# Writing out the engine loops of a graph network's three edge layers with constant addresses and waits

## The chip, the cores and the metric

The kernel runs on one core of one Trainium2 chip. The metric is the device time of one launch, in microseconds (us): lower is better. Three runs of the kernel before gave 8099.27, 8096.51 and 8084.9 us, median 8096.51 us. The profile below is of a further execution, which took 8076.82 us.

## The reference

`x` is 3125 nodes by 128 features. There are 100000 edges `src -> dst`, sorted by `dst`, with 16 attributes and one weight each. Four graph networks run one after the other, each followed by a residual addition and a layer normalization: two attention convolutions, a mean aggregation, three edge layers, and a last attention layer. The change touches the third network alone:

```python
h = x @ W_enc + b_enc
ea = edge_attr @ W_ee + b_ee
for i in range(3):
    m = relu(h[src] + ea) * edge_atten
    aggr = segment_sum(m, dst, num_segments=n)
    z = (1.0 + eps[i]) * h + aggr
    z = z @ W1[i] + b1[i]
    z = (z - bn_mean[i]) * rsqrt(bn_var[i] + 1e-5) * bn_gamma[i] + bn_beta[i]
    h = relu(relu(z) @ W2[i] + b2[i])
```

## The kernel before, in words

The launch is a row of blocks. Up to about 3868 us come the index work, the two attention convolutions, the mean aggregation and the preparation of the edge layers. Then `gine_edges()` (line 1181) and `gine_nodes(layer)` (line 1282) alternate three times (lines 1523 and 1524), and the last network and the output follow. `gine_edges()` is the same code in all three layers.

One edge layer lays the 100000 edges on 128 partitions by J = 784 columns, so that a column is 128 edges and each partition holds edges that follow each other in `dst` order. Four columns are a quad (196 of them, `QUADS`), sixteen are a turn of the loops (`RUN` = 16, 49 turns). Five instruction streams work side by side:

- POOL (`@block.gpsimd`, line 1199) gathers, one column per indirect DMA, the rows `h[src]` from the DRAM table `h_tab` into a ring of 16 columns, that is 4 quads. Before quad q it waits until DVE has used quad q - 4 (`z_done`, q - 3). This stream is written out in full already, 784 gathers per layer.
- ACT copies a 128 by 128 block of edge attributes (line 1217) and, after PE has transposed it (line 1231), copies it back from PSUM (line 1220). PE multiplies the block with `W_ee` laid out for 8 columns (line 1235), two matrix products for two quads. The quad's bank is free again when DVE has used it.
- DVE, line 1263: waits for the quad's gather and its product and adds them into `z`, 128 by 512.
- DVE, line 1268, one per column: `m = max(z, 0) * weight`.
- DVE, line 1256, one per column: a running sum along the partition, `run = run_before * same + m`, where `same` is 0 at the first edge of a node. Each waits for the one before it (`run_done`) and for its `m` (`m_done`). The running sums of a quad are issued between the `m` operations of the quad after it.
- SP (line 1208) writes each 8 finished columns, 512 KB, to `run_tab` in DRAM. DVE waits for that before it uses the 8 places again (`run_out`).

The order on DVE is written by hand: `step(i, u, behind)` is one quad, `runs(i, u, k)` one running sum. DVE writes out the first four quads (the call `step(0, u, u > 0)`) and then runs a loop (`Fori`, line 1272) of 48 turns of four quads. SP loops over all 49 turns (line 1205), ACT and PE over turns 1 to 48 (lines 1222 and 1237). Inside a loop the turn's number is a register: addresses (`bass.ds(...)`) and the values that waits compare with are worked out by register instructions of the engine's own queue. `later()` (its wait is at line 77) is a wait that is left out where its constant is 0 or less.

The node stage that follows reads the running sum of each node's last edge from `run_tab` and applies the two products of the layer.

Of the kernel before, what the change touches and what calls it, by code (L numbers as in the profile page):

```python
# [17 lines left out]
ALU = mybir.AluOpType  # L18
# [3 lines left out]
P = 128  # L22
N = 3125
E = 100000
D = 128
# [6 lines left out]
J = -(-E // (P * 16)) * 16  # L32
# [47 lines left out]
def build(nc, a, out):  # L80
    ctx = ExitStack()
    with ctx:
# [1098 lines left out]
        def gine_edges():  # L1181

            with ExitStack() as ph:
# [7 lines left out]
                with nc.Block() as block:  # L1191
# [10 lines left out]

                    @block.sync
                    def _(sp):
                        with nc.sync.Fori(0, J // RUN) as i:
                            for h in range(2):
                                sp.wait_ge(run_done, RUN * i + 8 * h + 8)
                                sp.dma_start(run_rows[:, bass.ds((RUN * i + 8 * h) * D, 8 * D)], run[:, 8 * h * D:8 * (h + 1) * D]).then_inc(run_out[h], 16)
                        for h in range(2):
                            sp.wait_ge(run_out[h], 16 * J // RUN)  # L1210

                    @block.scalar
                    def _(act):
                        def sixteen(i):
                            for u in range(2):
                                later(act, tr_done, 2 * i + u - 1)
                                nc.scalar.copy(stage[u], ea_nat[:, bass.ds((2 * i + u) * P, P)]).then_inc(staged, 1)
                                act.wait_ge(tr_done, 2 * i + u + 1)
                                later(act, mm_done, 4 * i + 2 * u - 2)
                                nc.scalar.copy(ea_T[u], bank[6 + u][:, 0:P]).then_inc(copied, 1)  # L1220
                        sixteen(0)
                        with nc.scalar.Fori(1, J // RUN) as i:
                            sixteen(i)

                    @block.tensor
                    def _(pe):
                        def sixteen(i):
                            for u in range(2):
                                pe.wait_ge(staged, 2 * i + u + 1)
                                later(pe, copied, 2 * i + u - 1)  # L1230
                                nc.tensor.transpose(bank[6 + u][:, 0:P], stage[u], ident[:, :]).then_inc(tr_done, 1)
                                pe.wait_ge(copied, 2 * i + u + 1)
                                later(pe, z_done, 4 * i + 2 * u - 2)
                                for k in range(2):
                                    nc.tensor.matmul(bank[2 * u + k][:, :], ea_T[u], w_blocks[:, k * 512:(k + 1) * 512], start=True, stop=True).then_inc(mm_done, 1)  # L1235
                        sixteen(0)
                        with nc.tensor.Fori(1, J // RUN) as i:
                            sixteen(i)

                    @block.vector  # L1240
                    def _(dve):
# [6 lines left out]
                        def runs(i, u, k):  # L1248

                            t = 16 * i + 4 * u + k  # L1250
                            slot = 4 * u + k
                            dve.wait_ge(m_done, t + 1)
                            later(dve, run_done, t)
                            if k == 0 and u % 2 == 0:
                                later(dve, run_out[u // 2], 16 * i)
                            nc.vector.scalar_tensor_tensor(run[:, slot * D:(slot + 1) * D], run[:, (slot - 1) % RUN * D:((slot - 1) % RUN + 1) * D],  # L1256
                                                           same_nat[:, bass.ds(t, 1)], m_of(u)[:, k * D:(k + 1) * D], ALU.mult, ALU.add).then_inc(run_done, 1)

                        def step(i, u, behind):
                            q = 4 * i + u  # L1260
                            dve.wait_ge(slot_in[u], 64 * (i + 1))
                            dve.wait_ge(mm_done, q + 1)
                            nc.vector.tensor_tensor(z_of(u), bank[u][:, :], ring[:, u * 512:(u + 1) * 512], ALU.add).then_inc(z_done, 1)  # L1263
                            for k in range(4):
                                if behind:
                                    runs(i if u > 0 else i - 1, (u - 1) % 4, k)
                                dve.wait_ge(z_done, q + 1)
                                nc.vector.tensor_scalar(m_of(u)[:, k * D:(k + 1) * D], z_of(u)[:, k * D:(k + 1) * D], 0.0,  # L1268
                                                        weight_nat[:, bass.ds(16 * i + 4 * u + k, 1)], ALU.max, ALU.mult).then_inc(m_done, 1)
                        for u in range(4):  # L1270
                            step(0, u, u > 0)
                        with nc.vector.Fori(1, J // RUN) as i:
                            for u in range(4):
                                step(i, u, True)
                        for k in range(4):
                            runs(J // RUN - 1, 3, k)

# [361 lines left out]
```

## Time and profile before

| what | us |
|---|---|
| median of three runs | 8096.51 |
| the profiled execution | 8076.82 |
| its span in the trace | 8075.1 |
| edge layer 1, first gather to last running sum | 3869.5 to 5059.6 |
| edge layer 2 | 5138.5 to 6328.5 |
| edge layer 3 | 6404.3 to 7587.3 |
| busy in the span: DVE / POOL / PE / ACT | 4330.2 / 4213.9 / 3659.2 / 866.8 |

Busy time counts the work on an engine's datapath. Register, branch and wait instructions are not busy: they stand in the trace under the engine's queue, with a q behind its name (DVEq, SPq). Idle time ahead of an instruction is put down to whoever ended it. "issue" means that the profile shows nobody: the instruction was not there yet.

### The profile page before, as it was taken

Reading aid. Unit: us, or ns where it says so; the run is one execution under the profiler, and the core shown is the slowest. Engines: PE = TensorE matmul, PEld = TensorE weight load, DVE = VectorE, ACT = ScalarE, POOL = GpSimd, SP = SyncE. Lnnn points to the kernel's source line nnn. Section 1 sums busy time; section 2 is a strip of 40 time slices with the busy share of each in tenths; the row PEclk is TensorE's granted clock in tenths of the full one; section 3 lists DMA queues with packets and bytes.
Section 4 is the critical chain, followed back from the end, with each engine's and each line's share of the span. In section 5 each row is a group of like instructions: output and inputs, shape, how many; then the busy total and the mean of one; then the engine's idle time right before and its main releaser. Section 6 shows DMA issues by size and latency. Waiting matters only on the chain. (4 is left out here: it accounts for less than half of the span.)

```text
span 8075.1 us, 75499 instructions
## 1 busy us (share of the span) xinstructions
PE 3659.2 (45%) x15737; PEld 2363.8 (29%) x15739; DVE 4330.2 (54%) x9443; ACT 866.8 (11%) x2809; POOL 4213.9 (52%) x4279
## 2 busy tenths in 40 slices
PE   4366666663666666655222322332322323322244
PEld 2254444442444444455110101111110101100144
DVE  5455555554555555576444444344444344544478
ACT  0011111110111111101000000000000000000043
POOL 0455555533555555410566666466666466666443
PEclk7555555565555555577556555565566665566677
DMA  1454555524555454364322222222222222222264
GB/s 30 138 147 141 145 149 145 146 79 122 149 145 145 142 148 140 109 258 168 100 85 87 88 85 87 69 89 85 87 87 85 70 87 85 90 86 87 65 238 187
DMA packets 571997, 943.76 MB, mean 117 GB/s; under 512 B 90581, under 2 KB 413611, under 8 KB 558680
## 3 DMA queue, kind: packets, MB, share of 16 engines
q0 software_dynamic: 173728, 545.15, 22.4%
q1 hardware_dynamic: 398008, 395.34, 15.7%
q8 instruction: 139, 2.28, 0.1%
q14 instruction: 122, 1.00, 0.0%
HBM read 619.47 MB, written 320.66 MB: 116 GB/s over the span
## 5 line engine op out<-in xcount | busy, mean ns | idle before, releaser
L1199 POOL DMA_INDIRECT big<-h_tab,big x2352 | 2237.8, 951 | 1420.0 <-issue 799.3
L622 POOL DMA_INDIRECT big<-kv_tab,big x1664 | 1617.4, 972 | 1330.7 <-DVE big L788 867.6
L1235 PE MATMUL psum<-big 128*128 128x512 f32 x1176 | 969.8, 973 | 2505.4 <-DVE big L1263 2062.1
L1256 DVE SCALAR_TENSOR_TENSOR big<-big 128x128 f32<-128x128 f32 x2352 | 827.2, 352 | 1274.0 <-issue 1233.8
L1235 PEld LDWEIGHTS psum<-big 128*128 128x128 f32 x1176 | 308.5, 290 | 3013.9 <-issue 2253.8
L740 PE MATMUL psum<-big 128*128 128x136 f32 x3328 | 931.4, 433 | 488.8 <-issue 417.1
L740 PEld LDWEIGHTS psum<-big 128*128 128x128 f32 x3328 | 781.9, 315 | 642.2 <-issue 605.1
L696 PE MATMUL psum<-big 128*128 x4992 | 713.3, 296 | 408.9 <-issue 408.7
L1268 DVE TENSOR_SCALAR big<-big 128x128 f32<-128x128 f32 x2352 | 718.0, 306 | 311.3 <-issue 261.8
L783 DVE TENSOR_TENSOR big<-psum,big 128x512 f32<-128x512 f32 x416 | 287.5, 691 | 851.9 <-PE psum L696 554.9
L702 PE MATMUL psum<-big 128*128 128x128 bf16 x1408 | 577.7, 410 | 216.1 <-ACT big L661 112.6
L696 PEld LDWEIGHTS psum<-big 128*128 128x128 bf16 x4992 | 454.2, 120 | 711.6 <-issue 671.7
L661 ACT COPY big<-psum 125x128 f32<-125x128 f32 x1408 | 376.3, 267 | 2444.5 <-PE psum L702 1517.0
L1263 DVE TENSOR_TENSOR big<-psum,big 128x512 f32<-128x512 f32 x588 | 404.3, 688 | 299.7 <-issue 199.7
L1220 ACT COPY big<-psum 128x128 f32<-128x128 f32 x294 | 77.9, 265 | 3312.5 <-issue 1555.2
L1459 POOL DMA_INDIRECT big<-snap_tab,small x100 | 215.3, 2153 | 397.1 <-DVE big L1468 218.3
L819 DVE SCALAR_TENSOR_TENSOR big<-big,psum 128x136 f32<-128x136 f32 x832 | 294.5, 354 | 204.0 <-PE psum L740 81.7
L702 PEld LDWEIGHTS psum<-big 128*128 128x128 bf16 x1408 | 227.4, 161 | 306.8 <-issue 258.5
L788 DVE TENSOR_TENSOR big<-big 128x512 f32<-128x512 f32 x416 | 284.1, 683 | 0.5 <-ACT big L669 0.5
L796 DVE TENSOR_TENSOR big<-big,small 128x512 f32<-128x512 f32 x416 | 284.2, 683 | 0.0
L793 DVE TENSOR_REDUCE big<-big 128x32 f32<-128x512 f32 x416 | 282.8, 680 | 0.7
L1496 PE MATMUL psum<-skip,big 128*128 128x128 f32 x1250 | 183.7, 320 | 110.3 <-DVE big L1474 110.3
(374 smaller groups left out, 3359.9 us busy)
## 6 DMA issues: line engine op xcount, KB each, us to landing
run_tab<-big SPq DMA_DIRECT2D x294, 512.0 KB
snap_tab<-big SPq DMA_DIRECT2D x352, 224.0 KB
item_tab<-big SPq DMA_DIRECT2D x208, 272.0 KB
big<-loc_tab SPq DMA_DIRECT2D x104, 512.0 KB
big<-h_tab,big POOLq DMA_INDIRECT x2352
big<-kv_tab,big POOLq DMA_INDIRECT x1664
snap_tab<-big SPq DMA_DIRECT2D x352, 26.0 KB
kv_tab<-big SPq DMA_DIRECT2D x10, 640.0 KB, 3.3
```

The costliest lines, as they stand in the source:

```text
L622: nc.gpsimd.indirect_dma_start(out=kv[:, b % SLOTS, k, :], out_offset=None, in_=kv_tab, in_offset=bass.IndirectOffsetOnAxis(ap=src_item[:, ...
L661: nc.scalar.copy(snaps[0:125, n % 8 * P:(n % 8 + 1) * P], bank[7][0:125, 0:P]).then_inc(snapped, 1)
L696: ins_ = nc.tensor.matmul(bank[b % 2][:, k * P:(k + 1) * P], hot_T[b // 4 % 2][:, (b % 4 * 4 + k) * P:(b % 4 * 4 + k + 1) * P], q3[:, bass ...
L702: nc.tensor.matmul(bank[7][:, 0:P], key_hot[n // 8 % 2][:, n % 8::8], lo_hot[n // 8 % 2][:, n % 8::8], start=first_c + n == 0, stop=True, ...
L740: ins_ = nc.tensor.matmul(region(2 * b + i), hot[b % 2][:, k * P:(k + 1) * P], va[b % 2][:, k, :], start=s == 0, stop=s == 1)
L783: nc.vector.tensor_tensor(prod[t % 2].rearrange("p (k c) -> p k c", c=D), bank[t % 2][:, :].rearrange("p (k c) -> p k c", c=D), kv[:, t % ...
L819: nc.vector.scalar_tensor_tensor(run[:, i % 8, :], run[:, (i - 1) % 8, :], keep[:, i:i + 1], region(i), ALU.mult, ALU.add).then_inc(run_do ...
L1199: nc.gpsimd.indirect_dma_start(out=ring[:, slot * D:(slot + 1) * D], out_offset=None, in_=h_tab, in_offset=bass.IndirectOffsetOnAxis(ap=sr ...
L1235: nc.tensor.matmul(bank[2 * u + k][:, :], ea_T[u], w_blocks[:, k * 512:(k + 1) * 512], start=True, stop=True).then_inc(mm_done, 1)
L1256: nc.vector.scalar_tensor_tensor(run[:, slot * D:(slot + 1) * D], run[:, (slot - 1) % RUN * D:((slot - 1) % RUN + 1) * D], same_nat[:, bas ...
L1263: nc.vector.tensor_tensor(z_of(u), bank[u][:, :], ring[:, u * 512:(u + 1) * 512], ALU.add).then_inc(z_done, 1)
L1268: nc.vector.tensor_scalar(m_of(u)[:, k * D:(k + 1) * D], z_of(u)[:, k * D:(k + 1) * D], 0.0, weight_nat[:, bass.ds(16 * i + 4 * u + k, 1)] ...
```

## The change

All `Fori` loops of `gine_edges()` become Python loops, on SP, ACT, PE and DVE. Every address and every wait value becomes a constant. On DVE the wait for `z_done` stands only ahead of a quad's first `m`, and the wait for `m_done` only ahead of a quad's first running sum, where it asks for all four `m` of the quad. Each engine issues the same work in the same order, POOL's code is untouched, and so is everything outside `gine_edges()`.

```diff
                     @block.sync
                     def _(sp):
-                        with nc.sync.Fori(0, J // RUN) as i:
+                        for i in range(J // RUN):
                             for h in range(2):
                                 sp.wait_ge(run_done, RUN * i + 8 * h + 8)
-                                sp.dma_start(run_rows[:, bass.ds((RUN * i + 8 * h) * D, 8 * D)], run[:, 8 * h * D:8 * (h + 1) * D]).then_inc(run_out[h], 16)
+                                sp.dma_start(run_rows[:, (RUN * i + 8 * h) * D:(RUN * i + 8 * h + 8) * D], run[:, 8 * h * D:8 * (h + 1) * D]).then_inc(run_out[h], 16)
...
-                                nc.scalar.copy(stage[u], ea_nat[:, bass.ds((2 * i + u) * P, P)]).then_inc(staged, 1)
+                                nc.scalar.copy(stage[u], ea_nat[:, (2 * i + u) * P:(2 * i + u + 1) * P]).then_inc(staged, 1)
...
-                        sixteen(0)
-                        with nc.scalar.Fori(1, J // RUN) as i:
+                        for i in range(J // RUN):
                             sixteen(i)
...
-                        sixteen(0)
-                        with nc.tensor.Fori(1, J // RUN) as i:
+                        for i in range(J // RUN):
                             sixteen(i)
...
-                            dve.wait_ge(m_done, t + 1)
+                            if k == 0:
+                                dve.wait_ge(m_done, t + 4)
                             later(dve, run_done, t)
...
-                                                           same_nat[:, bass.ds(t, 1)], m_of(u)[:, k * D:(k + 1) * D], ALU.mult, ALU.add).then_inc(run_done, 1)
+                                                           same_nat[:, t:t + 1], m_of(u)[:, k * D:(k + 1) * D], ALU.mult, ALU.add).then_inc(run_done, 1)
...
-                                dve.wait_ge(z_done, q + 1)
+                                if k == 0:
+                                    dve.wait_ge(z_done, q + 1)
                                 nc.vector.tensor_scalar(m_of(u)[:, k * D:(k + 1) * D], z_of(u)[:, k * D:(k + 1) * D], 0.0,
-                                                        weight_nat[:, bass.ds(16 * i + 4 * u + k, 1)], ALU.max, ALU.mult).then_inc(m_done, 1)
-                        for u in range(4):
-                            step(0, u, u > 0)
-                        with nc.vector.Fori(1, J // RUN) as i:
-                            for u in range(4):
-                                step(i, u, True)
+                                                        weight_nat[:, 4 * q + k:4 * q + k + 1], ALU.max, ALU.mult).then_inc(m_done, 1)
+                        for q in range(QUADS):
+                            step(q // 4, q % 4, q > 0)
```

## Rows read from the trace of the kernel before

**Rows 1.** Page, costliest groups: the gathers and the three DVE lines.
```profile
L1199 POOL DMA_INDIRECT big<-h_tab,big x2352 | 2237.8, 951 | 1420.0 <-issue 799.3
L1256 DVE SCALAR_TENSOR_TENSOR big<-big 128x128 f32<-128x128 f32 x2352 | 827.2, 352 | 1274.0 <-issue 1233.8
```

**Rows 2.** By stage: us, busy us of PE, PEld, DVE, ACT, POOL, clock, DMA.
```profile
3869.00:5060.00 1191.00, 341.49 (x489) 123.07 (x489) 574.93 (x1764) 49.71 (x195) 745.30 (x784) 0.59 0.28 86
...
6404.00:7588.00 1184.00, 329.23 (x489) 120.57 (x488) 564.88 (x1764) 49.49 (x193) 746.78 (x784) 0.60 0.28 86
...
5004.00:5019.00 15.00, 0.96 (x2) 0.00 (x0) 3.24 (x9) 0.56 (x2) 9.46 (x10) 0.50 0.19 49
5019.00:5027.00 8.00, 4.47 (x7) 1.90 (x8) 7.54 (x25) 0.46 (x2) 4.90 (x6) 0.71 0.37 132
```

**Rows 3.** Timeline of POOL in layer 1, one loop turn: start us, duration, line.
```profile
4996.44 1.00 POOL L1199 DMA_INDIRECT big<-h_tab,big  x1 [4.46 <-DVE big L1263]
...
5015.25 0.94 POOL L1199 DMA_INDIRECT big<-h_tab,big  x1 [0.30 <-issue]
5020.58 1.00 POOL L1199 DMA_INDIRECT big<-h_tab,big  x1 [4.38 <-DVE big L1263]
```

**Rows 4.** Who waited for POOL's ring, layer 1: total us, times, longest.
```profile
POOL big L1199 <- DVE big L1263: 211.0, 49, 6.4
```

**Rows 5.** DVE's queue in the slow stretch 5004 to 5019: min/median/max ns.
```profile
L1256 DVEq FUSED_REGOPS  x4: 683/695/708, 5005.0 to 5017.0; - x4
...
L77 DVEq EVENT_SEMAPHORE  x4: 14/352/701, 5005.0 to 5017.0; - x4
L1252 DVEq ALU_OP  x5: 3/686/703, 5003.6 to 5018.4; - x5
```

**Rows 6.** The same instructions 5019 to 5027, and 5047 to 5060 (last turn).
```profile
L1256 DVEq FUSED_REGOPS  x11: 4/57/57, 5019.1 to 5026.5; - x11
...
L1256 DVEq FUSED_REGOPS  x16: 57/57/57, 5047.0 to 5057.3; - x16
```

**Rows 7.** Timeline 3869 to 3895: the turn that DVE already has written out.
```profile
3869.47 0.96 POOL L1199 DMA_INDIRECT big<-h_tab,big  x1 [57.41 <-issue]
...
3873.23 0.94 POOL L1199 DMA_INDIRECT big<-h_tab,big  x1 [0.30 <-issue]
...
3875.84 0.69 DVE L1263 TENSOR_TENSOR big<-psum,big 128x512 f32<-128x512 f32 x1 [28.66 <-DMA big<-h_tab,big]
...
3880.77 0.69 DVE L1263 TENSOR_TENSOR big<-psum,big 128x512 f32<-128x512 f32 x1 [3.32 <-DMA big<-h_tab,big]
...
3881.97 1.03 POOL L1199 DMA_INDIRECT big<-h_tab,big  x1 [0.30 <-issue]
...
3889.64 0.94 POOL L1199 DMA_INDIRECT big<-h_tab,big  x1 [0.30 <-issue]
```

**Rows 8.** Waits in that written-out turn, 3870 to 3895; SP's loop, 3886 to 3895.
```profile
L77 DVEq EVENT_SEMAPHORE  x11: 21/21/21, 3881.8 to 3893.8; - x11
...
L1207 SPq ALU_OP  x1: 709/709/709, 3888.9 to 3888.9; - x1
```

**Rows 9.** Timeline, end of layer 1: last gather, last quad, last running sums.
```profile
5048.52 0.94 POOL L1199 DMA_INDIRECT big<-h_tab,big  x1 [0.30 <-issue]
...
5052.31 0.69 DVE L1263 TENSOR_TENSOR big<-psum,big 128x512 f32<-128x512 f32 x1
...
5055.13 0.69 DVE L1263 TENSOR_TENSOR big<-psum,big 128x512 f32<-128x512 f32 x1
...
5057.89 1.73 DVE L1256 SCALAR_TENSOR_TENSOR big<-big 128x128 f32<-128x128 f32 x4
```

**Rows 10.** Instructions of the gathers over the whole kernel; DVE's loop branch; instruction queues.
```profile
L1199 POOL DMA_INDIRECT big<-h_tab,big x2352: 938/944/1077, 3869.5 to 7573.4; - x196
...
L1272 DVEq COMPARE_BRANCH  x144: 1/56/721, 3930.6 to 7585.4; - x144
...
q8 instruction: 139, 2.28, 0.1%
```

## The prediction

> **What bounds the kernel now.** The change touches the three edge layers alone, so I read the groups of instructions first, then the engines by stage. A layer lasts some 1191 us; in it POOL is busy for 745 us and DVE for 575 us [rows 2], and neither is full. The groups say that both are short of something: the gathers sat idle for 1420 us over the three layers, the running sums for 1274 us, and nearly all of the latter has no releaser ("issue") [rows 1]. DVE was waiting for its own instructions.
>
> POOL's timeline gives the beat. From one wait to the next, 4996.44 to 5020.58, is a turn of 16 gathers: 24.14 us. The gathers of a turn start 1.25 us apart (0.94 busy and 0.30 between two), so sixteen of them are 20 us. The rest is one wait of some 4.4 us for line 1263 [rows 3]. There are 49 such waits in the first layer, 211 us [rows 4]. The ring of four quads is full and DVE has not freed the next one, so **DVE bounds the loop and POOL waits for it**.
>
> Why is DVE late? In 8 us, from 5019 to 5027, it is busy for 7.54 us over 25 instructions. In the 15 us before, it is busy for 3.24 us over 9 instructions [rows 2]. Its queue shows the cause: a register instruction takes 57 ns in the quick stretch [rows 6] and some 695 ns in the slow one, and the waits at line 77 and the register sums at line 1252 reach 701 and 703 ns as well [rows 5]. Each turn holds such a stretch. What makes an instruction cost 0.7 us no row tells. But three rows tell where it does and doesn't happen. It is absent in the last turn, when POOL has no more gathers to issue [rows 6]. It is absent in the first turn of the layer, with gathers under way all the time: there DVE's code is already written out, and its 11 waits take 21 ns each, all of them. At 3888.9, within that same turn, SP, which runs a loop from the start, takes 709 ns for one register sum [rows 8]. So the slow dispatch needs gathers under way and hits looping streams. The written-out one beside it is spared.
>
> **The change, part by part.** *DVE's loop.* Its first turn is a sample of the code to come: quads follow each other at POOL's pace, 3875.84 to 3880.77, 4.93 us for four gathers [rows 7]. If the 48 other turns go like it, DVE needs per quad what it needs in the last turn, 5052.31 to 5055.13, 2.82 us [rows 9], against POOL's 5.0. It then waits for the gather, and POOL for nobody.
>
> *What is late next: POOL.* The sixteen gathers from 3869.47 to 3889.64 took 20.17 us, 1.261 us each [rows 7]. I take that and not the 1.249 us of an undisturbed pair, because in the first turn the odd gather costs 1.03 us where DVE works beside it, and DVE will now work beside every quad. The bounds: 1.249, if it costs nothing; 1.34, if each gather took 1.03 busy and 0.30 idle, as the disturbed one does. Layer: 783 intervals x 1.261 = 987 us.
>
> *The tail.* Now the last running sum ends 5059.6, 11.1 us after the last gather's start [rows 9]. Then: the quad's sum starts 2.6 us after its last gather does (3873.23 to 3875.84 [rows 7]), one quad of DVE work is 2.8 us, and four last running sums are 1.73 us [rows 9]. Sum 7.1 us. New layer 987 + 7 = 994 us. The layers now take 1190.1, 1190.0 and 1183.0 us, 3563 us together. **Saved: 3563 - 3 x 994 = 581 us.**
>
> *The two dropped waits.* They are instructions of DVE's queue or ride on one, at 21 to 57 ns. With DVE ahead of POOL they are hidden: worth nothing by themselves. If DVE stayed the bound, they would count (see the rivals). The wait for all four `m` costs nothing: the last of them is issued ahead of the next quad's 0.69 us addition [rows 7], which covers it.
>
> *SP, ACT and PE.* Their loops become constants too. PE and ACT are idle for most of a layer, busy 341 and 50 us of 1191 [rows 2]: nothing. SP's write starts a little sooner; DVE waits for it half a turn later, nothing. POOL's stream is unchanged. Its queue has no new work.
>
> *Fetching the longer code.* DVE's stream grows to 11 instructions a quad (9 of datapath, some 2 waits), 2156 a layer, where the loop held them once. The queue of instructions of the whole kernel shows 139 packets at 0.1% of the span of 16 engines, about 0.9 us each [rows 10]. Low end nothing; high end, a dozen in a layer and each in full on the path, 11 us a layer. DVE has 2.2 us to spare in each quad, so I take nothing.
>
> The Trainium skill, page "Runtime: NRT & Kernel Launch", section "Instruction fetch mechanics", says that a loop whose target lies within the two fetched pages (512 instructions) needs no fetch, and that only a branch beyond them stalls. By it the loop, about 107 instructions a turn, would cost nothing and its removal would bring nothing but the register instructions. The sum would be that of the second rival below. The row disagrees in part: the branch itself takes 56 ns [rows 10], as the rule has it, but instructions later in the turn take 0.7 us [rows 5], which the rule does not foresee.
>
> **The sum.** Against the profiled execution: 8076.8 - 581 = 7496 us. The median of the runs lies 19.7 us above that execution, so 7516 us. Ends of POOL's pace: 1.249 gives 9 us less in each layer, 7488; 1.34 gives 62 us more in each, 7701. About 0.2% (16 us) is what a measurement of this kernel can tell from no change.
>
> **Rivals.**
>
> *A. The slow dispatch comes with the gathers, whatever the code, but lets go when POOL pauses.* For it: the last turn, a loop too, is quick once POOL is done [rows 6]. Against it: the first turn. Price: in the slow stretch 9 datapath and some 17 queue instructions took 15 us, 0.58 us each [rows 2, 5]. Eleven a quad make 6.3 us, slower than POOL's 5.0. But a quick stretch of 8 us and three quads follows each pause of POOL. With a slow stretch T, DVE does T / 6.3 + 3 quads, POOL (T + 8 - 4.3) / 5: T is about 55 us, the cycle about 63 us with 11.7 quads, 5.4 us a quad. Layer 196 x 5.4 + 7 = 1065 us, saved 368 us: 7728 us. Here the dropped waits and register sums pay, since each instruction less is 0.58 us.
>
> *B. The slow stretch is a matter of time and not of instructions,* for example of something that POOL does every 24 us; writing the code out changes nothing: 8097 us. For it: the turn's regularity, and the rule above. Against it: each slow instruction costs the same 0.7 us, which looks like a cost per instruction, and the first turn.
>
> *C. Slower: the written-out stream is dispatched slowly without a pause.* Place: DVE's queue in all 196 quads, price 0.58 us an instruction. Then a quad takes 11 x 0.58 = 6.4 us against 6.07 now (1190 / 196), 1254 + 7 us a layer, 220 us more in three: 8317 us. It decides from 0.55 us an instruction, if no quick stretch relieves it. For it: only that in the slow stretch plain waits are slow as well [rows 5]. Against it: rows 8, where such waits take 21 ns.
>
> *D. POOL is slowed by a DVE that never pauses.* The Trainium skill, page "SBUF — State Buffer", section "SBUF: two separate sides", says that certain DVE operations lock the port pair that POOL shares, and that descriptors of gathers can't be written meanwhile. By that rule each gather would be held up by the DVE operation it meets. The trace shows the size: the longest of 2352 gathers took 1.077 us, the median 0.944 [rows 10]. All at 1.077 would be 1.38 us apart: 1079 + 7 us a layer, saved 305 us, 7792 us. It can't make the kernel slower than before, and in the first turn only the odd gather is disturbed.
>
> **How the numbers follow.** POOL-bound at 7516: 0.79. A: 0.10. B: 0.03. C: 0.03. D at its full price: 0.05. The POOL-bound case runs from 7488 (undisturbed pace) to some 7560 (every second gather disturbed); with an allowance of 10 us for the runs' own scatter the low end is 7478. To hold 8 in 10 with the parts of that case beyond 7560 I reach to A: 7478 to 7728. Faster by over 0.2%: main, A and D, 0.94. Within: B, 0.03. Slower: C, 0.03.
>
> **What the profile after would show.** Right: the idle time of the gathers behind line 1263 gone, from 49 waits to a handful; POOL busy for three quarters of a layer; gathers 1.25 to 1.27 us apart through the whole layer; DVE waiting for the gather ahead of line 1263, some 2 us a quad; no wait in DVE's queue near 0.7 us; layers of about 994 us. Wrong: waits in DVE's queue with a median near 0.7 us beside POOL waits (A, or C if every layer is over 1191 us); a turn of still 24 us (B); gathers with a mean of 1.03 us or more (D).

## The result, and the profile after

The kernel after takes 7872.89 us, the median of four runs (7868.31 to 7887.57); the kernel before took 8090.7 us beside it. The ratio is 0.9734, with a 95% interval of 0.9716 to 0.9751: 218 us less, where 581 were forecast, and outside the forecast's range of 7478 to 7728 us. The profiled execution took 7871.88 us, 204.9 us less than that of before.

All of it lies in the three edge layers. From the first gather to the end of the last running sum they take 1119.9, 1116.8 and 1121.6 us, 205 us less in sum than the 3563 us of before. The forecast was 994 us each. The page of the kernel after, to be read against [rows 1]:

```profile
q8 instruction: 152, 2.49, 0.1%
q14 instruction: 178, 1.46, 0.1%
...
L1199 POOL DMA_INDIRECT big<-h_tab,big x2352 | 2249.1, 956 | 1201.3 <-issue 814.8
...
L1255 DVE SCALAR_TENSOR_TENSOR big<-big 128x128 f32<-128x128 f32 x2352 | 815.7, 347 | 1463.7 <-remote 1067.7
...
L1268 DVE TENSOR_SCALAR big<-big 128x128 f32<-128x128 f32 x2352 | 689.8, 294 | 156.2 <-remote 126.2
...
L1262 DVE TENSOR_TENSOR big<-psum,big 128x512 f32<-128x512 f32 x588 | 400.9, 682 | 190.7 <-DMA big<-h_tab,big 175.4
```

The gathers' idle time fell from 1420 to 1201 us, while the running sums' rose from 1274 to 1464 us. Most of the latter has only changed its name: "issue" before, "remote" now (a wait whose semaphore was updated just before, by nobody that the profile shows). With nothing but 0.30 us between gathers, 2352 of them would leave some 710 us of idle time. So POOL still waits, as the engines by layer show [rows 2] and the gathers' own line confirms (duration minimum, median and maximum in ns, then first and last start):

```profile
3865.00:4985.00 1120.00, 344.17 (x489) 125.32 (x489) 525.35 (x1763) 45.12 (x195) 749.92 (x784) 0.61 0.30 92
5062.00:6180.00 1118.00, 348.18 (x489) 126.64 (x489) 528.48 (x1764) 44.71 (x193) 750.17 (x784) 0.61 0.30 92
6256.00:7378.00 1122.00, 342.12 (x489) 124.25 (x487) 525.19 (x1764) 44.73 (x193) 749.03 (x784) 0.61 0.30 91
```

```profile
L1199 POOL DMA_INDIRECT big<-h_tab,big x784: 938/944/1143, 3865.7 to 4971.3; - x196
its engine sat idle before it (us, times) until:
  issue: 292.6, 744
  remote: 102.1, 33
  DVE big L1262: 19.3, 7
```

783 intervals between gathers in 1105.6 us are 1.412 us each, where 1.261 was forecast. 744 of the 784 follow at once; 40 wait, 121 us together, in place of 49 waits of 211 us [rows 4].

**The slow hand-over is still there**, in the written-out code. DVE's timeline in the first layer, at its first appearance and later on (start, duration, what released it in brackets):

```profile
3897.91 0.69 DVE L1262 TENSOR_TENSOR big<-psum,big 128x512 f32<-128x512 f32 x1 [3.25 <-DMA big<-h_tab,big]
3898.52 0.34 DVE L1255 SCALAR_TENSOR_TENSOR big<-big 128x128 f32<-128x128 f32 x1
...
3899.99 0.35 DVE L1255 SCALAR_TENSOR_TENSOR big<-big 128x128 f32<-128x128 f32 x1 [0.47 <-DVE big L1255]
...
3902.79 0.35 DVE L1255 SCALAR_TENSOR_TENSOR big<-big 128x128 f32<-128x128 f32 x1 [2.13 <-remote]
...
3907.00 0.35 DVE L1255 SCALAR_TENSOR_TENSOR big<-big 128x128 f32<-128x128 f32 x1 [3.06 <-remote]
3908.43 0.30 DVE L1268 TENSOR_SCALAR big<-big 128x128 f32<-128x128 f32 x1 [1.07 <-issue]
```

```profile
4490.57 0.68 DVE L1262 TENSOR_TENSOR big<-psum,big 128x512 f32<-128x512 f32 x1
...
4493.03 0.68 DVE L1262 TENSOR_TENSOR big<-psum,big 128x512 f32<-128x512 f32 x1
...
4510.90 0.69 DVE L1262 TENSOR_TENSOR big<-psum,big 128x512 f32<-128x512 f32 x1
...
4522.21 0.68 DVE L1262 TENSOR_TENSOR big<-psum,big 128x512 f32<-128x512 f32 x1
4525.93 0.35 DVE L1255 SCALAR_TENSOR_TENSOR big<-big 128x128 f32<-128x128 f32 x1 [3.04 <-issue]
4527.33 0.28 DVE L1268 TENSOR_SCALAR big<-big 128x128 f32<-128x128 f32 x1 [1.05 <-remote]
4528.76 0.35 DVE L1255 SCALAR_TENSOR_TENSOR big<-big 128x128 f32<-128x128 f32 x1 [1.14 <-remote]
4529.02 0.38 DVE L1268 TENSOR_SCALAR big<-big 128x128 f32<-128x128 f32 x1
4530.86 0.38 DVE L1255 SCALAR_TENSOR_TENSOR big<-big 128x128 f32<-128x128 f32 x1 [1.45 <-issue]
4531.16 0.27 DVE L1268 TENSOR_SCALAR big<-big 128x128 f32<-128x128 f32 x1
4532.99 0.35 DVE L1255 SCALAR_TENSOR_TENSOR big<-big 128x128 f32<-128x128 f32 x1 [1.56 <-remote]
...
4533.45 0.68 DVE L1262 TENSOR_TENSOR big<-psum,big 128x512 f32<-128x512 f32 x1
4537.89 0.35 DVE L1255 SCALAR_TENSOR_TENSOR big<-big 128x128 f32<-128x128 f32 x1 [3.75 <-remote]
4538.59 0.28 DVE L1268 TENSOR_SCALAR big<-big 128x128 f32<-128x128 f32 x1 [0.35 <-remote]
```

A slow quad, 4510.90 to 4522.21, takes 11.3 us; a quick one 2.5 (4490.57 to 4493.03). "remote" and "issue" hide one thing: the `m` operations that carry no wait (4529.02, 4531.16) follow at once, while the running sums and the first `m` of a quad, which carry one, come late, though what they wait for is long done. Over the three layers none of 1328 `m` operations without a wait starts over 0.3 us late, and 932 of 2302 running sums do. Two facts stand out. The first stretch begins at 3899.99, 34 us after the layer's first gather (34 and 30 us in the other two layers). And the late starts lie on a grid: from 4525.93 on the distances are 1.40, 1.43, 2.10, 2.13, 4.90 and 0.70 us, within 0.03 us multiples of 0.70. POOL starved meanwhile: its timeline has

```profile
4533.41 0.94 POOL L1199 DMA_INDIRECT big<-h_tab,big  x1 [0.30 <-issue]
4538.82 0.94 POOL L1199 DMA_INDIRECT big<-h_tab,big  x1 [4.47 <-remote]
```

### The profile page after: what moved, and what is told of

The parts are those of the page before. It is cut to its first block and busy times, and to the rows that moved or that the text cites. A ratio compares the mean times of both kernels' runs of the same rounds, so it can differ in the third digit from the quotient of the medians.

```text
span 7870.1 us, 63617 instructions
## 1 busy us (share of the span) xinstructions
PE 3674.0 (47%) x15737; PEld 2367.2 (30%) x15739; DVE 4198.5 (53%) x9443; ACT 852.5 (11%) x2809; POOL 4226.3 (54%) x4279
## 5 line engine op out<-in xcount | busy, mean ns | idle before, releaser
L1234 PE MATMUL psum<-big 128*128 128x512 f32 x1176 | 987.3, 989 | 2262.8 <-remote 1226.0
L1268 DVE TENSOR_SCALAR big<-big 128x128 f32<-128x128 f32 x2352 | 689.8, 294 | 156.2 <-remote 126.2
```

## Experiments

The runs came in six groups. Those of one group ran on one chip, each beside the kernel before. The groups differ: the kernel before took 7147 and 7155 us in two of them (chips numbered 7 and 13) and 7977 to 8091 us in all others (chips numbered 0, 6, 0, 6, and the result above, whose chip has no number on record). No chip number was seen in both conditions, but each of the two quick ones was seen once only, so "chip" below is the likely, not the proven, name of what differs. Below, "layer" is a layer's time from its first to its last gather, and "time lost" is what POOL's intervals over 1.7 us have beyond 1.25 us each, summed over a layer. A late start is one of DVE's operations other than line 1262 with over 0.6 us of idle time ahead of it.

**First group: a chip on which the kernel before takes 7147.23 us.** `waits_back` is the kernel after with both repeated waits:

```diff
-                            if k == 0:
-                                dve.wait_ge(m_done, t + 4)
+                            dve.wait_ge(m_done, t + 1)
...
-                                if k == 0:
-                                    dve.wait_ge(z_done, q + 1)
+                                dve.wait_ge(z_done, q + 1)
```

> The loops written out as in the change, but with the two repeated waits put back ahead of every running sum and every m operation. Theory 1 (in the slow stretches each instruction that DVE's queue has to dispatch costs some 0.6 to 1.1 us, whatever the form of the code, so the gain is that of fewer instructions): three more wait instructions a quad, a slow quad longer by about 1 us, and since POOL's pauses soak up part of it some 10 to 40 us slower than the change, 7885 to 7915 us. Theory 2 (the gain comes from getting rid of the loop's branch and registers alone): no difference, 7873 us.

Measured: 7145.6 us, 0.9996 (0.9986 to 1.0005). `loops_fewer_waits` is the other half alone, the kernel before with the same four lines turned round (loops kept, waits dropped):

> The kernel before, with its loops, and only the two repeated waits dropped. Theory 1: fewer instructions in the queue for each column (the wait for m on three of four running sums; the wait for z rides on an address computation that stays), so 20 to 60 us faster than before, 8030 to 8070 us. Theory 2: no difference from before, 8091 us.

Measured: 7137.83 us, 0.9984 (0.9974 to 0.9994). Neither half makes a difference here, and the traces say why: there is no slow hand-over to remove. The gathers and the running sums of `waits_back`, then the register instructions ahead of the running sums in the looping `loops_fewer_waits`:

```profile
L1199 POOL DMA_INDIRECT big<-h_tab,big x2352 | 2248.5, 956 | 812.3 <-issue 812.3
...
L1254 DVE SCALAR_TENSOR_TENSOR big<-big 128x128 f32<-128x128 f32 x2352 | 811.3, 345 | 5.4 <-DVE big L1266 4.4
```

```profile
L1257 DVEq FUSED_REGOPS  x2304: 57/57/57, 3587.0 to 6648.0; - x192
```

All 2304 of them take 57 ns; in the same kernel's run of the third group the same line has a maximum of 1442 ns. From the first gather to the last, the written-out layers take 987 us, exactly the 783 x 1.261 of the forecast, and the looping ones 979 to 981 us: POOL-bound in both forms. The chip's attention stages are shorter too; the edge layers start at 3565 us here and at 3866 us in the kernel after.

`one_m` makes the four `m` operations of a quad one operation of 128x512, so that DVE has 6 operations a quad and not 9:

```diff
-                                dve.wait_ge(m_done, t + 4)
+                                dve.wait_ge(m_done, t // 4 + 1)
...
                                 if k == 0:
                                     dve.wait_ge(z_done, q + 1)
-                                nc.vector.tensor_scalar(m_of(u)[:, k * D:(k + 1) * D], z_of(u)[:, k * D:(k + 1) * D], 0.0,
-                                                        weight_nat[:, 4 * q + k:4 * q + k + 1], ALU.max, ALU.mult).then_inc(m_done, 1)
+                                    nc.vector.scalar_tensor_tensor(m_of(u).rearrange("p (k d) -> p k d", d=D), z_of(u).rearrange("p (k d) -> p k d", d=D), 0.0,
+                                                                   weight_nat[:, 4 * q:4 * q + 4].unsqueeze(2).to_broadcast([P, 4, D]), ALU.max, ALU.mult).then_inc(m_done, 1)
```

> The change, with the four m operations of a quad (128 by 128 each) replaced by one over 128 by 512, the same values. Theory 1: DVE's quad falls from 9 to 6 datapath instructions; in a slow stretch it takes about 8 us where it took about 11.7, so POOL pauses less often: about 5.45 us a quad on average instead of 5.64, some 110 us faster than the change, 7740 to 7790 us, with POOL waiting fewer than 35 times a layer instead of 40 to 49. Theory 2, or DVE bound by its datapath: within 20 us of the change, since the datapath's busy time hardly changes.

Measured: 7192.14 us, 1.0055 (1.0036 to 1.0073), layers of 1001 to 1002 us. The gathers' mean rises from 956 to 974 ns beside the wider operation. `paced` adds, after each gather, a small memset on POOL and the wait for it:

```diff
                                     in_offset=bass.IndirectOffsetOnAxis(ap=src_nat[:, 4 * q + k:4 * q + k + 1], axis=0)).then_inc(slot_in[q % 4], 16)
+                                if k % 1 == 1 - 1:
+                                    pause(nc.gpsimd.memset(small[:, 1100:1164], 0.0))
```

> The change, with a small memset of unused memory on POOL after every gather and a wait for it, so that gathers start some 0.2 to 0.4 us further apart. Theory 3 (what makes dispatch slow builds up while gathers follow each other without a pause and drains in pauses): the slow stretches get shorter or vanish, first slow dispatch later than 30 us after the layer's first gather, DVE waits for gathers, and the layer is POOL's pace times 783, 1150 to 1300 us. Rival (slow dispatch comes with any gather under way, however spaced): the slow stretches stay, POOL still waits 40 times a layer for line 1262 and the layer is longer than its pace times 783 by over 80 us.

Measured: 7528.63 us in a single run, layers of 1110 us (under the expected 1150 to 1300, as the memset costs less than assumed), and no late start. Here it tells the two theories apart in nothing; it is the yardstick for the same kernel further down.

**Second group: a chip on which the kernel before takes 8047.73 us.** The kernels before and after once more, and `one_m`:

> The kernel before, unchanged, for its trace beside the runs of this call. Theory 4 (slow dispatch on DVE's and SP's queues is a property of the chip or of its surroundings, and not of the kernel): either some 7145 us with no register instruction near 0.7 us and no wait of POOL's ring, or some 8090 us with both, and nothing between.

> The change, unchanged. Where the kernel before takes some 7145 us: POOL bounds both, each gather 1.261 us after the last beside the denser DVE stream, so within 0.2% of before or up to 30 us slower. Where it takes some 8090 us: 7873 us again, 2.7% faster. A rival by which the change gains from its form alone expects it faster by over 100 us on either chip.

> The change with one m operation a quad. Where before takes some 7145 us: 40 to 50 us slower than before, as in the first call. Where it takes some 8090 us: theory 1 (cost per dispatched instruction) expects 7740 to 7790 us; if only the datapath counts, 7855 to 7895 us.

Measured: 8045.6; 7855.8, 0.9757 (0.9742 to 0.9772); 7834.48, 0.9731 (0.9716 to 0.9746). The slow hand-over is back, with layers of 1170 to 1174, 1104 to 1106 and 1099 to 1100 us. `one_m` missed both of its expectations (7740 to 7790 and 7855 to 7895 us): three operations fewer saved 5 us a layer.

**Third group: before 8072.56 us.** The two halves again, where they can tell something:

> The change with the two repeated waits put back, once more, since the chip of the first call (before at 7147 us) shows no slow dispatch. Theory 5 (DVE dispatches some 70 to 80 instructions quickly after a pause of POOL and then about 0.7 to 1 us each until POOL's next pause): a quad has 14 instructions instead of 11, so the quick stretch lasts some 5 quads instead of 7, and the kernel lands between the change and before: where before takes some 8050 to 8090 us, 20 to 80 us slower than the change. A rival (the repeated waits cost nothing, only the form of the code counts): within 15 us of the change. Where before takes some 7147 us: 0.9996 of it again.

> The kernel before with only the repeated waits dropped, once more. Where before takes some 8050 to 8090 us, theory 5: fewer instructions a turn, 20 to 80 us faster than before. The rival (form alone): the same as before. Where before takes some 7147 us: 0.998 of it again.

Measured: 7869.5, 0.9749 (0.9733 to 0.9766), and 8062.81, 0.9984 (0.9974 to 0.9993). So **the repeated waits are worth nothing or next to it, and writing the code out is worth the whole gain**. `one_m_drain8` is `one_m` and lets POOL wait every 8 quads until the ring is empty:

```diff
-                                pool.wait_ge(z_done, q - 3)
+                                pool.wait_ge(z_done, q if q % 8 == 0 else q - 3)
```

> One m operation a quad, and POOL waits ahead of every eighth quad until DVE has added all quads issued so far, a pause of some 3 us every 40. Where before takes some 8050 to 8090 us, theory 5: eight quads are 64 instructions, the quick stretch never runs out, no slow dispatch, a layer is 196 quads of 5.05 us plus 24 pauses of 3.3 us, 1065 to 1080 us instead of 1106 to 1112, so 60 to 130 us faster than one m alone, 7700 to 7780 us. If the pause does not renew anything (slow dispatch comes at its own times): 1120 us a layer or more, 7850 us or more. Where before takes some 7147 us: the pauses are pure loss, 24 x 3.3 = 80 us a layer, 7420 us.

> The change with a small memset after every gather. Where before takes some 8050 to 8090 us: if any small gap on POOL lets DVE fetch its instructions, dispatch stays quick and the layer is 783 x 1.41 = 1104 us plus 7; if only a pause of some us does, the slow stretches stay and the layer is over 1150 us. Where before takes some 7147 us: 7529 us as in the first call.

Measured: 7951.98 us, 0.9843 (0.9824 to 0.9862), layers of 1132 to 1142 us, for the first. Late starts are fewer with the planned pauses, 138 to 180 a layer against 362 to 384 in `one_m` of the second group, but they cost more than they give: the 24 of them take 120 to 130 us of POOL's time where all of `one_m`'s waits cost 86 to 89. And a short pause doesn't always end a slow stretch. POOL stood still from 4523.42 to 4525.99 in one whose late starts run from 4522.25 to beyond 4571:

```profile
4522.39 1.03 POOL L1199 DMA_INDIRECT big<-h_tab,big  x1 [0.30 <-issue]
4525.99 1.39 POOL L1199 DMA_INDIRECT big<-h_tab,big  x1 [2.57 <-DVE big L1262]
```

`paced`, a single run, took 7883.67 us with layers of 1116 to 1117 us. That is nearly the 1110 us of the chip without the slow hand-over, and POOL waits for DVE four times in 2352 gathers:

```profile
L1200 POOL DMA_INDIRECT big<-h_tab,big x2352: 946/952/1142, 3867.0 to 7385.4; - x196
its engine sat idle before it (us, times) until:
  issue: 575.7, 1541
  POOL small L1204: 224.7, 807
  DVE big L1265: 0.8, 3
  remote: 0.3, 1
```

DVE's late starts fall from 271 to 296 a layer in the kernel after to 78, 9 and 33. At 1.41 us a gather the slow hand-over all but goes.

**Fourth group: before 7976.95 us. Which engine's loop, what sets the place, are the stores needed.** `only_vector` writes out DVE alone, with the repeated waits kept; `vector_loop` keeps DVE's loop alone (its code of the kernel before, with the waits dropped).

> The kernel before with DVE's loop alone written out (constant addresses and waits on DVE, both repeated waits kept); SP, ACT and PE keep their loops. Theory 6, the gain is on DVE alone (its register and wait instructions no longer pass through its own queue at 0.5 us each while the dispatch is slow): ratio to the kernel before 0.973 to 0.977, as with everything written out, layers of about 1105 us from the first gather to the last. Rival: the gain comes from fewer instructions being handed over on the chip as a whole (SP's, ACT's and PE's register instructions among them): 0.985 to 0.99, layers of about 1140 us. A second rival, SP's stores set when the slots of the running sums come free: no gain, 1.00.

> The kernel after with DVE's loop put back (registers for its addresses and waits, the two repeated waits still dropped); SP, ACT and PE stay written out. Theory 6: ratio to the kernel before 0.997 to 1.001, layers of about 1175 us, as e9_loops_fewer_waits. Rival, fewer instructions on the whole chip: 0.985 to 0.99. Second rival, SP's stores: 0.975.

Measured: 7825.94 us, 0.9808 (0.9787 to 0.983), layers 1103 to 1107 us; and 7969.45 us, 0.9992 (0.9979 to 1.0006), layers 1151 to 1156 us. DVE's loop is what costs: with it alone the kernel is as slow as with all four, without it the layers are the expected 1105 us, up to 5 us over those of `shifted` below. The ratio 0.9808 lies over the expected 0.977, and `vector_loop`'s layers are shorter than the expected 1175 us. The kernel before is 71 us quicker here than in the second group, though both ran on a chip numbered 0. No trace of it from this group shows how much of that lies in its layers; the first gather comes at 3820 to 3831 us here and at 3847 to 3858 us there, so some of it lies ahead of them.

```diff
...
+                        for j in range(48):
+                            nc.vector.memset(small[:, 1100 + j:1101 + j], 0.0)
                         for q in range(QUADS):
                             step(q // 4, q % 4, q > 0)
```

> The kernel after with 48 one-column memsets on DVE ahead of the first z of each layer. They cost about 3 us a layer, most of it while DVE waits for the first gathers. In the kernel after the first slow stretch of a layer lies at operations 51 to 84 of DVE counted from the layer's first z, in each of the three layers (36 to 65 us after the first gather). Theory 7, the place in DVE's stream of instructions decides: the stretch moves forward by 48 operations, to about 3 to 36. Rival, what POOL has done since the layer's start decides (33 us of gathers one behind the other): it stays at 51 to 84, at 30 to 40 us after the first gather. The time says little here: 0.972 to 0.98 of the kernel before under either.

> The kernel after with SP storing one of each eight columns of running sums (the output is no longer the reference's: seven eighths of the running sums are not stored; the table is filled with zeros ahead of each layer by 49 plain stores of 1 MB, some 150 us a layer or less, before the first gather). Theory 8, the slow dispatch needs the 512 KB stores of SP, which run beside the gathers: no slow stretches, layers of about 987 us from the first gather to the last. Rival, it comes with the gathers alone: layers of 1095 to 1110 us, the first slow stretch at operations 51 to 84 as in the kernel after.

`shifted` (above), a single run: 7809.87 us, layers 1098 to 1102 us. Counted in DVE's operations from the layer's first `z`, the first start over 0.4 us late is operation 49, 40 and 40 in the three layers, 30 to 35 us after the first gather; in the kernel after, counted alike, it is 47, 44 and 40. (The 51 to 84 of the expectation come from another count.) It did not move by 48, so the place in DVE's stream of instructions doesn't set it. `small_stores`, a single run, stores one column in eight and leaves out the rest: layers 1099 to 1103 us, 7918.82 us with the added plain stores. Seven eighths of the stores' bytes less change nothing, so their volume has no part; as many stores are issued as before.

**Fifth group: before 7978.4 us.** `m_on_act`, by far the largest relief for DVE: 5 operations a quad and not 9.

```diff
...
+                            act.wait_ge(z_done, q + 1)
+                            nc.scalar.activation(z, z, ACT.Relu).then_inc(r_done, 1)
+                            act.wait_ge(r_done, q + 1)
+                            later(act, run_done, 4 * q - 4)
+                            for k in range(4):
+                                nc.scalar.activation(m[:, k * D:(k + 1) * D], z[:, k * D:(k + 1) * D], ACT.Copy, scale=weight_nat[:, 4 * q + k:4 * q + k + 1]).then_inc(m_done, 1)
...
```

> The kernel after with the messages m = relu(z) * weight made on ACT (one Relu over 128x512 and four copies of 128x128 scaled by the weight column) and not by four operations of DVE, so that DVE hands over z and four running sums a quad: 5 operations where the kernel after has 9. Theory 9, what is left of the gap is the hand-over of DVE's operations at 1.0 to 1.4 us each in the slow stretches: a slow quad takes about 5 x 1.2 = 6 us and not 9 to 12, against POOL's 5.0, so the pauses of POOL nearly go and a layer takes 995 to 1060 us from the first gather to the last (1105 in the kernel after); the ratio to the kernel before is 0.94 to 0.96. Rival, the stretches grow as they did with one m operation and give it back: layers of 1090 or more, 0.97 to 0.975. Second rival, ACT's hand-over becomes slow too when it has more to do: DVE waits for m, 0.98 or more. On a chip without the slow hand-over every one of them says 0.998 to 1.003.

> The kernel after itself, for the same chip as e16_m_on_act: 0.973 to 0.98 of the kernel before where the slow hand-over exists, 0.998 to 1.002 where it does not (by the two runs on the chip where the kernel before takes 7147 us).

Measured: 7809.67 us, 0.9788 (0.9771 to 0.9804), against 7809.18 us, 0.9789 (0.9773 to 0.9805), of the kernel after. Layers 1100 to 1101 us against 1098 to 1100: the same, with DVE busy for 394 us of a layer where it was 525:

```profile
3833.00:4945.00 1112.00, 387.16 (x490) 125.52 (x490) 394.01 (x980) 400.82 (x1175) 743.47 (x784) 0.58 0.30 92
```

Its timeline in a slow stretch shows DVE, PE and ACT late together:

```profile
4332.35 1.51 DVE L1269 SCALAR_TENSOR_TENSOR big<-big 128x128 f32<-128x128 f32 x4 [2.65 <-remote]
4333.06 1.28 ACT L1221 ACTIVATE big<-big 128x128 f32<-128x128 f32 x4 [2.70 <-remote]
...
4338.65 1.51 DVE L1269 SCALAR_TENSOR_TENSOR big<-big 128x128 f32<-128x128 f32 x4 [4.19 <-remote]
...
4340.07 0.47 PE L1244 MATMUL psum<-ident,big 128*128 128x128 f32 x1 [10.92 <-issue]
...
4342.17 3.78 PE L1248 MATMUL psum<-big 128*128 128x512 f32 x4 [1.63 <-ACT big L1229]
...
4343.56 1.28 ACT L1221 ACTIVATE big<-big 128x128 f32<-128x128 f32 x4 [2.19 <-issue]
...
4348.45 1.52 DVE L1269 SCALAR_TENSOR_TENSOR big<-big 128x128 f32<-128x128 f32 x4 [7.69 <-remote]
```

From start to start: 0.71, 5.59, 1.42, 2.10, 1.39, 4.89 us, or nearly 1, 8, 2, 3, 2 and 7 times 0.70, across three engines. The running sums at 4348.45 wait for messages that ACT had finished at 4344.8. Theory 9 fell, and so did the premise that ACT is never slow: both rivals hold in part. The slow quads are shorter, 16.8 us for two (4340.08 to 4356.91), but there are more of them: 77 to 83 of a layer's 195 quads take over 6.3 us, where in the kernel after of this group 62 to 67 do.

**What all these runs have in common.** On the chips with the slow hand-over:

| form | layer, us | time lost, us | mean per gather, us |
|---|---|---|---|
| before (result and second group) | 1169 to 1179 | 185 to 196 | 1.50 |
| loops, fewer waits | 1172 to 1178 | 182 to 190 | 1.50 |
| DVE's loop alone | 1151 to 1156 | 160 to 168 | 1.47 |
| after (result, second and fifth group) | 1098 to 1108 | 111 to 121 | 1.41 |
| DVE alone written out, waits kept | 1103 to 1107 | 115 to 119 | 1.41 |
| after, waits back | 1106 to 1110 | 120 to 124 | 1.41 |
| one m operation | 1099 to 1100 | 86 to 89 | 1.40 |
| one m operation, planned pauses | 1132 to 1142 | 131 to 142 | 1.45 |
| m on ACT | 1100 to 1101 | 118 to 120 | 1.41 |
| paced | 1116 to 1117 | 12 to 16 | 1.43 |

Of the 12 to 16 us of `paced`, 11 are there in its run on the quick chip as well.

Whatever DVE has to do, written-out code without pauses of its own ends at 1.40 to 1.41 us a gather: two steps of 0.70. It looks as if these chips kept up with no more than one gather in 1.405 us, and POOL, issuing at 1.25, ran ahead until the engines' waits were served late and the full ring stopped it. The last run was to test that at a pace between the two (the memset after every second gather):

> The kernel after with a small memset and its wait on POOL after every second gather, so that gathers follow each other at 1.25 and 1.39 us in turn, 1.32 in the mean. Theory 10, the chip keeps up with one gather in about 1.405 us in the long run (1100 us / 783) and POOL's pauses are what it gives back: the layers stay at 1098 to 1112 us whatever POOL's own pace, its pauses lose (1.405 - 1.32) x 783 = 60 to 75 us in place of 112 to 120, and the ratio to the kernel before is 0.973 to 0.982. Rival, a gap on POOL in itself clears the hand-over: 783 x 1.32 + 10 = 1044 us, ratio 0.95 to 0.96. Second rival, the pause lost stays at 115 us and the slower pace adds to it: 1034 + 115 = 1149 us, ratio 0.99 to 1.0.

It is the sixth group. It ran on a chip where the kernel before takes 7155.11 us and no start is late: 7328.68 us, 1.0238 (1.0221 to 1.0255), layers of 1044 us. That is 783 x 1.333, POOL's own pace, and tells the theories apart in nothing.

**Two rivals that the traces bear on.** *Slower transfers?* No: the packets take as long in the kernel after as in `waits_back` on the first chip. Within the layers the mean is 130 against 126 ns in the gathers' queue, 148 against 147 ns in that of the stores, and 416 against 406 and 1068 against 1105 ns in the two queues of instructions (q14 and q8). *The recording?* This one is open. `prof` answers for the gathers of `waits_back` on the first chip (the line of the kernel after, asked alike, has no such row):

```profile
DMA to landing us min/median/max: 2.4/2.5/3.7
```

On the quick chips the trace holds some 14045 records of DMAs landing between a layer's first and last gather, on the others 1069 to 2647: most are missing. In the kernel after's first layer they thin out from 87 to 29 to 12 in the first three stretches of 10 us, before DVE's first late start, where `waits_back` on the first chip has 109, 124 and 139. The three layers of `paced` on the slow chip hold 3694, 8581 and 5253, with 78, 9 and 33 late starts: the fewer late starts, the more records. (From kernel to kernel it is not in proportion: `m_on_act` has the fewest records, 1069 to 1092, with 110 to 123 late starts of DVE.) So the loss of records and the slow hand-over come together. Whether one brings the other, and whether a launch that records nothing has either, no run shows: for every time on record the span and the granted clock of the core were recorded too.

## Why the prediction was wrong

**The step that failed** is "If the 48 other turns go like it": the sample was taken too early. The first turn was quick because it came first; that it was written out did not protect it. Its gathers end 20 us after the layer's first one [rows 7]. DVE's stretches begin 29 to 36 us after it, in the kernel before (loops) as in the kernel after (34 us at 3899.99). So "the written-out one beside it is spared" was read from a time in which no trace has a late start of DVE, whatever its code. What came in its place: a slow quad of 11.3 us where 2.82 were taken, and POOL, which was to wait "for nobody", lost 117 to 121 us a layer waiting for DVE. That is nearly all of the 125 us between 994 and the 1119 us measured in the mean. The slow SP instruction at 3888.9 [rows 8] was the warning: at that moment something was slow already.

**What bounds the kernel before, and POOL's pace**: right. Without its pauses POOL issues every 1.261 to 1.264 us in the kernel after, against 1.261 forecast; on the first chip the layer was 987 us, as forecast. The price of DVE's disturbance (rival D) is small: mean 956 ns, longest 1143.

**A quad of written-out code on DVE, 2.82 us**: right in quick stretches (2.5 us), too low in slow ones (11.3 us in the one shown).

**The tail**, 7.1 us: in `waits_back` on the first chip it is 7.3 to 7.4 us. In the kernel after it is 14.3 us in the first layer (4971.3 to 4985.6) and 9.8 and 13.7 us in the others, as DVE has a backlog there.

**The dropped waits, nothing**: right as a number (0.9749 with them, 0.9734 and 0.9757 without, on chips with a like kernel before). Rival A's clause that each instruction less pays 0.58 us is refuted. SP, ACT and PE, nothing: right within some 5 us a layer (`only_vector` against `shifted`). Fetching, nothing: the queues of instructions carry 152 and 178 packets, and on the first chip the longer code costs at most 8 us a layer (987 against 979 to 981 us).

**Rival A** was the nearest, with 0.10, 7728 us and layers of 1065 us. Its mechanism came, in part: the hand-over is slow in written-out code too, and after about two thirds of POOL's waits no start is late for 5 us (in the kernel before, after nearly all of them). Its price was too low by half, since 0.58 us an instruction came from a mean over datapath and register instructions: 11 a quad would be 6.3 us, and 11.3 were seen. But a right price would not have saved it as a model. It makes the layer follow DVE's instruction count, and the counts of `one_m` and `m_on_act` moved nothing. **Rival B**, no change, and C, slower, did not happen. The Trainium skill, "Runtime: NRT & Kernel Launch", section "Instruction fetch mechanics", lets a taken branch stall only where its target lies outside the fetched window, so by it a near loop costs nothing. On the first chip the loop indeed costs nothing that shows; in the fourth group DVE's loop costs (1153 - 1100) / 49, about 1.1 us a turn.

**What is shown and what is not.** Shown: the gain comes from DVE's written-out code; the waits and the volume of SP's stores have no part; the slow hand-over is there in some groups of runs only and reaches DVE, ACT, PE and SP; it nearly goes at 1.41 us a gather. Argued only: that it is a limit of 1.405 us a gather. The table speaks for it. The planned pauses speak against its simple form, since they should have been free and cost 33 to 42 us a layer beside `one_m` in another group. Open: what takes the 0.70 us, whether the recording has a part in it, why an instruction of a loop adds to it, and what sets the quick chips apart.

**No version beats the kernel after everywhere.** `one_m` gives 0.9731 against 0.9757 in the second group, where the intervals overlap, and costs 0.55% on the first.

## What to carry to other kernels

A stretch of a trace that runs free of a stall acquits its code only if the stall could have come then: compare it with the same moment of the other form, not with a later one. Where an engine is idle behind waits that were satisfied long ago, fewer or shorter operations may buy nothing; change the rate of whatever runs beside it (here the gathers) and see whether the loss moves. And a gain of this kind seems to belong to the chip: the same edit was worth 2.1 to 2.7% on some chips and, by its two halves, nothing on another, so look at the same instruction's duration on both before telling a cause. Last, count what a trace should hold (here some 14045 landings a layer, 16 for each of 882 DMAs less a few): where records are missing, ask whether the recording takes part in what it shows.

## What was not expected of the hardware

All of this was seen in recorded executions alone.

- The register instructions of one line take 57 ns throughout on one chip and up to 1442 ns on another, in the same program (`loops_fewer_waits`); the whole kernel before takes 7147 to 7155 or 7977 to 8091 us accordingly.
- In a slow stretch of `m_on_act` the late starts of DVE, ACT and PE lie on a common grid of 0.70 us; DVE's do in the kernel after too.
- In written-out code, operations of the datapath that carry no wait are not late (0 of 1328 `m` operations). Running sums that each wait for the one before them are not late when they stand side by side (four in 1.51 us at 4338.65 of `m_on_act`), but often are when an `m` stands between (932 of 2302).
- Indirect DMAs of 128 rows follow each other in 1.25 us (4525.91 to 4533.41 in the kernel after) while DVE is late beside them.
